# Perceiver block on one core: thirteen attention units a batch instead of fourteen, the left-over token done apart on transposed scores

## The chip, the cores and the metric

The kernel runs on one core of a Trainium2 chip. The metric is device time in microseconds (us). The engines are PE (TensorE, matmuls), ACT (ScalarE), DVE (VectorE), POOL (GpSimd) and SP (SyncE, which issues most DMAs). Each works through its own program in order and meets the others only at semaphores.

## The reference, cut to what matters

Sixteen batches. Each has 64 latents and 1601 context tokens of 128 channels. A cross attention with 16 heads reads the tokens and the latents themselves as keys; a small self attention and a mixture of experts follow, once, over all 1024 latents.

```python
x = layer_norm(ctx, g1, b1); l = layer_norm(latents, g2, b2)      # 1601 and 64 rows a batch
q = l @ Wq; k, v = split(concat([x, l]) @ Wkv)                     # 1665 keys
w = softmax((q * s) @ (k * s).T)                                    # per head, s = 64 ** -0.25
out = (w @ v) @ Wo
x = x + out                                                         # then self attention, experts
```

## The kernel before

**What is computed.** The key and value maps are folded into the queries and into the output map, so the heads share the 128-channel tokens. A batch's queries are 1024 columns (16 heads by 64 latents). Tokens lie in 13 tiles of 128: twelve full ones (`FULL`) and one of 65 rows (`REST`). The latents as keys are a unit of their own with 64 rows, since their queries are other columns of `q_hi` and `q_lo` (from `COLS` on). So a batch has 14 units: `UNITS = TILES + 1`, `LAT = TILES`. Each operand is kept as a high and a low float16 part, and each product is three matmuls: high by high, low by high, high by low.

**A unit.** `scores(turn, u)` on PE writes keys by 1024 query columns into two of the four banks of `S`, with six matmuls of 512 columns. The latent unit has two more that add the shift row (L1982). ACT turns the scores into the exponentials, first to the float16 part `p_hi` (`exponentials_high`, L1721), then in full into the bank (`exponentials_full`, L1726). DVE subtracts one from the other (`low_part`, L1429), which gives `p_lo` and frees the two banks for `scores(u + 2)`. `weigh(turn, u)` on PE multiplies by the tokens, six matmuls of 512 columns, into the two banks `OA`; the latent unit's go to the two work banks `W`.

**A slot.** One slot is one batch: `slot(b)` on each engine. PE's order in unit u is `scores(b, u)`, the early items of `PLAN[u]`, `weigh(b, u - 2)`, and the late items. The last two units of a batch are weighed in units 0 and 1 of the next slot. Items: `q` (48 matmuls of 64 columns: the next batch's queries, in four quarters), `m` (32 pieces of the first, rough score pass of the next batch, whose row maxima DVE takes; 24 long ones of 512 columns at L1942 and 8 short ones at L1944/L1945), `mt` (the maxima turned into a row), `pj` (96 matmuls, the output map of the batch before).

**Work banks.** The items take turns on two PSUM banks, `W[0]` and `W[1]`: `BANK` gives them out alternately in the order of `PLAN`. `bank_free(item)` has PE wait until the reader of the bank's item before has finished: DVE's `maxima` (L1417) for `m`, DVE's `queries_low` (L1408) for `q`, ACT's copies (L1735) for `ol`, the latent unit's output. So item n + 2 cannot start before item n was read. DVE's order in unit u is: statistics of batch b + 2 (L413, L403 to L409), `queries_low` and `maxima` of the unit's items, in unit 6 two short reciprocals (L704, L706), `low_part(b, u)`, in units 0 and 1 the high parts of batch b + 1 (L1302). ACT's is: `exponentials_high`, `queries_high` (L1707), `exponentials_full`, then in unit 0 the copy of `OA` (L1730), in unit 1 the copies of the latents' output (L1735), later the normalisation of raw tokens (L1659) and `o_hi` (L1702).

Of the kernel before, what the change touches and what calls it, by code (L numbers as in the profile page):

```python
# [29 lines left out]
UNITS = TILES + 1  # L30
LAT = TILES
HALF = COLS // 2
GROUPS = 4
# [46 lines left out]
def some(first, count):  # L80
# [7 lines left out]
        ([], []),  # L88
        ([("q", 0), ("q", 1)], some(0, 1)),
        (some(1, 2), some(3, 2)),  # L90
        ([("q", 2), ("q", 3)], some(5, 1)),
        (some(6, 2), some(8, 2)),
        (some(10, 2), some(12, 2)),
        (some(14, 2), some(16, 1)),
        (some(17, 2), some(19, 2)),
        (some(21, 2), some(23, 1)),
        (some(24, 2), some(26, 2)),
        (some(28, 2), some(30, 2)),
# [15 lines left out]
NORMALISE_AT = {6: [0], 7: [1, 2], 8: [3, 4, 5], 9: [6], 10: [7], 11: [8, 9], 12: [10, 11], 13: [12]}  # L114
RECIPROCALS_AT = 6
OUTPUTS_HIGH_AT = {10: 0, 11: 1}
PREP = ("q", "m", "mt")


def rows_of(u):  # L120
    return 128 if u < FULL else (REST if u == FULL else NQ)


def perceiver(nc, x, ctx_in, ln1_g, ln1_b, ln2_g, ln2_b, Wq, Wkv, Wo, aWq, aWk, aWv, aWo,
              lq1, lk1, lq2, lk2, rms_scale, gate_w, gate_b, expert_w, expert_b, out):
    es = ExitStack()
    with es:
# [18 lines left out]
        def part(start, size, dt=F32):  # L146
# [37 lines left out]
        lk_odd = [sb(f"lk_odd{k}", [NQ, TB, D], F16) for k in range(2)]  # L184
# [5 lines left out]
        ck_hi = [sb(f"ck_hi{p}", [NQ, D], F16) for p in range(2)]  # L190
        ck_lo = [sb(f"ck_lo{p}", [NQ, D], F16) for p in range(2)]
# [4 lines left out]
        xT_hi = [sb(f"xT_hi{p}", [128, TILES * 128], F16) for p in range(2)]  # L196
        xT_lo = [sb(f"xT_lo{p}", [128, TILES * 128], F16) for p in range(2)]
# [101 lines left out]
                   (("q", 4), ("mt", 2), ("pj", 1))}  # L299
# [3 lines left out]
                "mt": sem("m_row", 2), "ol": sem("ol_copied", 2), "pj": sem("pj_copied", 1)}  # L303
# [22 lines left out]
        def pbuf(turn, u):  # L326
            return (2 * (turn.off % 2) + u) % NPB

        def score_bank(u, half):
            return S[:, 2 * (u % 2) + half, :]  # L330
# [111 lines left out]

        def inverse_rows(sp, turn):
# [66 lines left out]
        X1_AT, H_AT, TILE0_AT, KEYS1_AT, VALUES1_AT = 2, 8, 10, 11, 12  # L510
# [31 lines left out]
        def early_variances(dve, link, u):  # L542
# [4 lines left out]
            if u == X1_AT + 1:  # L547
                for t in range(5):
                    nc.vector.bn_stats(st[:, t, :], xres[:, t, :])
# [485 lines left out]
        def tail_tensor(pe, side_item, weigh):  # L1035
# [114 lines left out]
            pe.wait_ge(lo_done.sem, lo_done.upto(LAST, TILES - 1))  # L1150
# [3 lines left out]
            weigh(LAST, TILES - 1)  # L1154
# [60 lines left out]
        def _(sp):  # L1215
# [25 lines left out]
            transposes(sp, Turn(0))  # L1241
            load_raw(sp, Turn(2))
            sp.wait_ge(lk_done.sem, 1)
            for k in range(2):
                sp.dma_start(lk_odd[k][:], lk[k][NQ:128]).then_inc(ld_lk.sem, 16)
            for b in range(B):
                if b + 1 < B:
                    transposes(sp, Turn(b + 1))
                if b + 3 < B:
                    load_raw(sp, Turn(b + 3))  # L1250
                if b + 3 == B:
                    sp.dma_start(xres[:], x.rearrange("(t j) q d -> (j q) t d", j=2)).then_inc(ld_res.sem, 16)
                if b > 0:
                    inverse_rows(sp, Turn(b - 1))
            inverse_rows(sp, LAST)
# [9 lines left out]
        def _(dve):  # L1265
# [158 lines left out]
            def low_part(turn, u):  # L1424

                r, k = rows_of(u), pbuf(turn, u)
                dve.wait_ge(e_done.sem, e_done.upto(turn, u))
                src = S[0:r, 2 * (u % 2):2 * (u % 2) + 2, :].rearrange("p a n -> p (a n)")
                nc.vector.tensor_tensor(p_lo[k][0:r, :], src, p_hi[k][0:r, :], ALU.subtract)\  # L1429
                  .then_inc(lo_done.sem, 1)  # L1430

            def slot(b, prep=True, post=True, stats=True):
                nxt = b.plus(1)
                for u in range(UNITS):
                    if stats:
                        statistics(b.plus(2), u)
                    for kind, k in PLAN[u][0] + PLAN[u][1]:
                        if kind == "q" and prep:
                            queries_low(nxt, k)
                        if kind == "m" and prep:  # L1440
                            maxima(nxt, k)
                    if u == RECIPROCALS_AT and post:
# [54 lines left out]
        def _(pool):  # L1497
# [50 lines left out]
            def at_batch(k, turn):  # L1548
                return lk_odd[k][:, turn.off // 2, :] if turn.off % 2 else lk[k][0:NQ, turn.off // 2, :]
# [8 lines left out]
            def current_k(turn):  # L1558
# [3 lines left out]
                if turn.off == 1:  # L1562
                    pool.wait_ge(ld_lk.sem, 32)
                nc.gpsimd.tensor_copy(ck_hi[p][:], at_batch(0, turn))
# [549 lines left out]
```

## Time and profile before

| | us |
|---|---|
| median of 3 runs | 997.82 (996.78 to 1000.93) |
| the profiled execution, as timed | 998.82 |
| its span in the trace | 997.1 |
| PE busy | 944.7 (95%) |
| DVE busy | 782.8 (79%) |
| ACT busy | 738.6 (74%) |
| POOL busy | 376.0 (38%) |
| one slot in the steady part | 49.53 |

The span is from the first to the last instruction. A matmul's record of 512 columns lasts 380 ns, but the next one starts 216 ns after it began: records overlap, and a PE that has stood still for up to some 160 ns still looks busy. For PE one therefore reads the starts, not the busy time. The timeline merges equal neighbours; "x2" is two matmuls, and its start is that of the first.

### The profile page before, as it was taken

What the parts mean: (1) busy time and instruction counts of PE and PEld (TensorE: products, weight loads), DVE (VectorE), ACT (ScalarE), POOL (GpSimd) and SP (SyncE); (2) the same over time, 40 slices, a digit from 0 to 9 for tenths busy, and PEclk for the clock granted to TensorE, in tenths of its full rate; (3) what the DMA queues carried; (4) which work ended last, traced back from release to release, by engine and by line L of the source; (5) the groups of instructions that cost most, each with busy time, mean ns of one, the idle gap of its engine ahead of it and who ended that gap; (6) DMA issues with size and microseconds to landing.
All of it is one profiled execution on the core that took longest, in us unless ns stands there. A gap on an engine that the chain in (4) does not pass through costs nothing.

```text
span 997.1 us, 19671 instructions
## 1 busy us (share of the span) xinstructions
PE 944.7 (95%) x7942; PEld 501.6 (50%) x7942; DVE 782.8 (79%) x1540; ACT 738.6 (74%) x1017; POOL 376.0 (38%) x376
## 2 busy tenths in 40 slices
PE   8679999999999999999999999999999998969975
PEld 5434455454545454545454545454545454547742
DVE  5968796969696969696969696969695956658965
ACT  4576878787878787878787878787878776635631
POOL 6471143433333343434343434343434223143343
PEclk9799999999999999999999999999999999979987
DMA  6212020302020312121212121121212000000000
GB/s 204 68 22 58 11 79 15 76 17 74 18 73 18 73 17 73 23 68 25 66 24 67 23 68 33 59 37 54 32 48 35 22 2 22 1 23 23 2 7 16
DMA packets 73218, 41.79 MB, mean 42 GB/s; under 512 B 60932, under 2 KB 68520, under 8 KB 73128
## 3 DMA queue, kind: packets, MB, share of 16 engines
q1 hardware_dynamic: 72840, 39.49, 16.4%
q8 instruction: 63, 1.03, 0.4%
q10 hardware_dynamic: 288, 1.05, 0.3%
q14 instruction: 27, 0.22, 0.1%
HBM read 25.98 MB, written 0.59 MB: 27 GB/s over the span
## 4 chain that ended last, share of the span: by engine, by line
PE 81%; DVE 13%; ACT 2%; issue 2%; POOL 1%; DMA 1%; POOLq 0%; ACTq 0%; DVEq 0%
PE S L1977 10%; PE S L1985 9%; PE S L1979 9%; PE OA L2006 9%; PE OA L2008 9%; PE OA L2010 9%; PE WW L1942 8%; PE WW L1958 1%; PE WW L1960 1%; DVE mx L1417 1%; PE WW L1959 1%; PE WW L1929 1%; DVE amx L720 1%; PE WW L1931 1%; PE WW L1930 1%
## 5 line engine op out<-in xcount | busy, mean ns | idle before, releaser
L1429 DVE TENSOR_TENSOR region<-S,region 128x1024 f16<-128x1024 f32 (+1 forms) x224 | 272.1, 1215 | 107.5 <-ACT S L1726 106.8
L1721 ACT ACTIVATE region<-S,sigma 128x1024 f16<-128x1024 f32 (+1 forms) x224 | 250.3, 1117 | 121.4 <-PE S L1985 121.4
L1417 DVE TENSOR_REDUCE mx<-WW 128x1 f32<-128x512 f32 (+1 forms) x480 | 263.6, 585 | 29.9 <-PE WW L1942 21.2
L1726 ACT ACTIVATE S<-S,sigma 128x1024 f32<-128x1024 f32 (+1 forms) x224 | 244.1, 1090 | 0.0
L1977 PE MATMUL S<-region,xT_hi 128*128 128x512 f16 (+1 forms) x416 | 124.3, 380 | 3.4 <-DVE region L1429 2.2
L2006 PE MATMUL OA<-region,xk 128*128 128x512 f16 (+1 forms) x416 | 124.4, 381 | 0.0
L1985 PE MATMUL S<-region,xT_lo 128*128 128x512 f16 (+1 forms) x416 | 124.2, 380 | 0.0
L2008 PE MATMUL OA<-region,xk 128*128 128x512 f16 (+1 forms) x416 | 124.2, 380 | 0.0
L1979 PE MATMUL S<-region,xT_hi 128*128 128x512 f16 (+1 forms) x416 | 124.1, 380 | 0.0
L2010 PE MATMUL OA<-region,xk 128*128 128x512 f16 (+1 forms) x416 | 124.0, 380 | 0.0
L1942 PE MATMUL WW<-xT_hi,region 128*128 128x512 f16 x360 | 120.3, 380 | 1.6 <-DVE region L1408 0.9
L1543 POOL TENSOR_TENSOR xk<-raw,xk 128x508 f16<-128x508 f32 x64 | 62.5, 996 | 143.1 <-DVE xk L1302 143.1
L461 POOL TENSOR_TENSOR region<-region,rb 128x512 f32<-128x512 f32 x32 | 40.5, 1267 | 141.2 <-DMA rb<-inv_dram 141.2
L469 POOL TENSOR_TENSOR ew<-region,o_hi 128x1024 f16<-128x1024 f32 x32 | 68.1, 2128 | 64.2 <-ACT o_hi L1702 64.2
L1659 ACT ACTIVATE raw<-raw,smc 128x128 f32<-128x128 f32 (+1 forms) x187 | 84.0, 491 | 0.0
L1532 POOL TENSOR_TENSOR smc<-smc,mhalf 128x13 f32<-128x13 f32 x16 | 38.9, 2433 | 99.1 <-DVE smc L409 99.1
L1979 PEld LDWEIGHTS S<-region,xT_hi 128*128 128x128 f16 (+1 forms) x416 | 41.2, 99 | 49.1 <-issue 0.6
L1985 PEld LDWEIGHTS S<-region,xT_lo 128*128 128x128 f16 (+1 forms) x416 | 41.2, 99 | 48.9 <-issue 0.5
L2010 PEld LDWEIGHTS OA<-region,xk 128*128 128x128 f16 (+1 forms) x416 | 40.8, 98 | 49.4 <-issue 0.6
L2008 PEld LDWEIGHTS OA<-region,xk 128*128 128x128 f16 (+1 forms) x416 | 40.7, 98 | 49.5 <-issue 0.6
L1942 PEld LDWEIGHTS WW<-xT_hi,region 128*128 128x128 f16 x360 | 35.0, 97 | 50.8 <-DVE mx L1417 13.8
L413 DVE BATCH_NORM_STATS2 stc<-raw 128x6 f32<-128x128 f32 (+1 forms) x208 | 45.6, 277 | 15.2 <-ACT raw L1659 15.2
(296 smaller groups left out, 1728.3 us busy)
## 6 DMA issues: line engine op xcount, KB each, us to landing
raw<-ctx SPq DMA_DIRECT2D x16, 768.0 KB
rb<-inv_dram SPq DMA_DIRECT2D x16, 512.0 KB, 3.6
raw<-ctx SPq DMA_DIRECT2D x16, 32.5 KB
WO_lo<-L_xattn_Wq ACTq DMA_DIRECT2D x1, 512.0 KB, 3.9
WO_hi<-L_xattn_Wkv ACTq DMA_DIRECT2D x1, 512.0 KB, 4.8
lx<-x SPq DMA_DIRECT2D x1, 512.0 KB, 5.9
region<-L_xattn_Wo SPq DMA_DIRECT2D x1, 512.0 KB, 8.0
WO_hi<-L_xattn_Wkv SPq DMA_DIRECT2D x1, 512.0 KB, 8.9
```

The source lines that it names most:

```text
L1417: nc.vector.tensor_reduce(mx[:, r, c:c + 1], W[BANK[("m", n)]][:, 0:width], AX.X, ALU.max)\
L1429: nc.vector.tensor_tensor(p_lo[k][0:r, :], src, p_hi[k][0:r, :], ALU.subtract)\
L1659: ins = nc.scalar.activation(x_[0:r, t, :], x_[0:r, t, :], ACT.Identity, bias=smc[0:r, 2, t:t + 1], scale=smc[0:r, 1, t:t + 1])
L1721: nc.scalar.activation(p_hi[k][0:r, :], src, ACT.Exp, scale=sigma[0:r, 0:1])
L1726: nc.scalar.activation(src, src, ACT.Exp, scale=sigma[0:r, 0:1]).then_inc(e_done.sem, 1)
L1942: ins = mm(w, rows, xT_hi[p][:, 512 * c:512 * c + 512], start=True, stop=True)
L1977: mm(score_bank(u, k)[0:r], hi, q_hi[p][:, cols[k]], start=True, stop=False)
L1979: mm(score_bank(u, k)[0:r], hi, q_lo[p][:, cols[k]], start=False, stop=False)
L1985: ins = mm(score_bank(u, k)[0:r], lo, q_hi[p][:, cols[k]], start=False, stop=True)
L2006: mm(dst[k], hi, ph[0:r, cols[k]], start=first, stop=False)
L2008: mm(dst[k], hi, pl[0:r, cols[k]], start=False, stop=False)
L2010: ins = mm(dst[k], lo, ph[0:r, cols[k]], start=False, stop=last)
```

## The change

- The last tile keeps 64 of its 65 tokens (`KEPT`), and these and the 64 latents form one unit of 128 rows, unit 12. `UNITS` is 13.
- In its `scores` each step is a pair of matmuls, tokens and latents, with 64 weight columns each and the results in partitions 0 to 63 and 64 to 127 of one bank. In its `weigh` each step is a pair with 64 rows each, the tokens' into `OA`, the latents' into the work banks.
- `OA` is complete only with that unit, so the weighing of unit 12 in the next slot's unit 1 stands ahead of `scores(b, 1)`, and ACT's copy of `OA` waits for it.
- The 65th token: a new item `lf` (late in unit 2) computes its scores transposed, 16 matmuls with 128 weight columns and one or two data columns. DVE adds the three parts, ACT takes the exponential twice (unit 3), DVE subtracts (unit 4), a new item `lt` (late in unit 5) turns the 16 columns into rows, ACT copies them, SP moves them by three DMAs into one tile of three rows, and `weigh_left` (unit 10) adds them to `OA` by two matmuls of 512 columns. SP also fetches three rows of the token itself.
- With one unit less, `PLAN` packs the 32 `m` items into units 3 to 11, and the normalisation and three steps of the last slot move by up to one unit. POOL's copies of the latents go to partitions 64 to 127, the banks of `S` and the `p` buffers alternate over all units instead of within a batch.

```diff
-UNITS = TILES + 1
-LAT = TILES
+UNITS = TILES
+LAT = TILES - 1
+KEPT = REST - 1
+LEFT = FULL * 128 + KEPT
...
 PLAN = [([], []),
         ([], []),
-        ([], []),
-        ([("q", 0), ("q", 1)], some(0, 1)),
-        (some(1, 2), some(3, 2)),
-        ([("q", 2), ("q", 3)], some(5, 1)),
-        (some(6, 2), some(8, 2)),
-        (some(10, 2), some(12, 2)),
-        (some(14, 2), some(16, 1)),
-        (some(17, 2), some(19, 2)),
-        (some(21, 2), some(23, 1)),
-        (some(24, 2), some(26, 2)),
-        (some(28, 2), some(30, 2)),
+        ([], [("lf", 0)]),
+        ([("q", 0), ("q", 1)], some(0, 2)),
+        (some(2, 2), some(4, 2)),
+        ([("q", 2), ("q", 3)], some(6, 1) + [("lt", 0)]),
+        (some(7, 2), some(9, 2)),
+        (some(11, 2), some(13, 2)),
+        (some(15, 2), some(17, 2)),
+        (some(19, 2), some(21, 2)),
+        (some(23, 2), some(25, 2)),
+        (some(27, 2), some(29, 3)),
         ([("mt", 0), ("mt", 1)], [("pj", 0)])]
...
-NORMALISE_AT = {6: [0], 7: [1, 2], 8: [3, 4, 5], 9: [6], 10: [7], 11: [8, 9], 12: [10, 11], 13: [12]}
+NORMALISE_AT = {6: [0], 7: [1, 2, 3], 8: [4, 5, 6], 9: [7, 8, 9], 10: [10, 11], 11: [12]}
+LEFT_EXP_AT, LEFT_LOW_AT, LEFT_AT = 3, 4, 10
...
-        X1_AT, H_AT, TILE0_AT, KEYS1_AT, VALUES1_AT = 2, 8, 10, 11, 12
+        X1_AT, H_AT, TILE0_AT, KEYS1_AT, VALUES1_AT = 2, 8, 9, 10, 11
...
+        def left_columns(sp, turn):
+            p = turn.off % 2
+            if turn.off >= 2:
+                sp.wait_ge(pv_done.sem, pv_done.upto(turn.plus(-2), LEFT_AT - 1))
+            sp.dma_start(left_x[p][0:2, :], xk[p][KEPT:REST, :, FULL, :]).then_inc(left_x_in[p].sem, 16)
+            sp.dma_start(left_x[p][2:3, :], xk_hi[p][KEPT:REST, FULL, :]).then_inc(left_x_in[p].sem, 16)
+        def left_rows(sp, turn):
+            sp.wait_ge(free["lt"].sem, free["lt"].upto(turn))
+            if turn.off > 0:
+                sp.wait_ge(pv_done.sem, pv_done.upto(turn.plus(-1), LEFT_AT - 1))
+            for k, first in enumerate((0, 0, 8)):
+                sp.dma_start(left_row[k:k + 1, :].rearrange("o (r n) -> o r n", n=128), left_pT[first:first + 8, :])\
+                  .then_inc(left_row_in.sem, 16)
...
+            def left_scores(turn):
+                dve.wait_ge(pe_item["lf"].sem, pe_item["lf"].upto(turn))
+                parts = W[BANK[("lf", 0)]][:, 0:32].rearrange("p (r c) -> p r c", c=4)[:, :, 0:3]
+                nc.vector.tensor_reduce(left_s[:], parts, AX.X, ALU.add).then_inc(free["lf"].sem, 1)
+            def left_low_part(turn):
+                dve.wait_ge(left_exp.sem, left_exp.upto(turn))
+                nc.vector.tensor_tensor(left_p[:, 8:16], left_e[:], left_p[:, 0:8], ALU.subtract)\
+                  .then_inc(left_low.sem, 1)
...
+            def left_exponentials(turn):
+                act.wait_ge(free["lf"].sem, free["lf"].upto(turn))
+                nc.scalar.activation(left_p[:, 0:8], left_s[:], ACT.Exp, scale=sigma[:, 0:1])
+                nc.scalar.activation(left_e[:], left_s[:], ACT.Exp, scale=sigma[:, 0:1]).then_inc(left_exp.sem, 1)
...
             def outputs(turn):
-                act.wait_ge(pv_done.sem, pv_done.upto(turn, TILES - 1))
+                act.wait_ge(pv_done.sem, pv_done.upto(turn, LAT))
...
+                if kind == "lf":
+                    for r in range(8):
+                        rows = slice(128 * r, 128 * r + 128)
+                        mm(w[:, 4 * r:4 * r + 2], q_hi[p][:, rows], xT[p][:, :, LEFT], start=True, stop=True)
+                        ins = mm(w[:, 4 * r + 2:4 * r + 3], q_lo[p][:, rows], xT_hi[p][:, LEFT:LEFT + 1],
+                                 start=True, stop=True)
+                if kind == "lt":
+                    pe.wait_ge(left_low.sem, left_low.upto(turn))
+                    if turn is LAST:
+                        pe.wait_ge(x1_read.sem, 1)
+                    ins = mm(w[0:16, 0:128], left_p[:], ident16[:], start=True, stop=True)
...
                 if u < LAT:
-                    hi, lo, qc = xT_hi[p][:, 128 * u:128 * u + r], xT_lo[p][:, 128 * u:128 * u + r], 0
+                    at = slice(128 * u, 128 * u + 128)
+                    keys_of = [(slice(0, 128), xT_hi[p][:, at], xT_lo[p][:, at], 0)]
                 else:
-                    hi, lo, qc = cT_hi[p][:], cT_lo[p][:], COLS
+                    at = slice(128 * u, 128 * u + KEPT)
+                    keys_of = [(slice(0, KEPT), xT_hi[p][:, at], xT_lo[p][:, at], 0),
+                               (slice(KEPT, 128), cT_hi[p][:], cT_lo[p][:], COLS)]
...
+            def weigh_left(turn):
+                pe.wait_ge(left_x_in[turn.off % 2].sem, raw_loaded(turn))
+                pe.wait_ge(left_row_in.sem, turn.times(48, 48))
+                for k in range(2):
+                    mm(OA[:, k, :], left_x[turn.off % 2][:], left_row[:, HALF * k:HALF * k + HALF],
+                       start=False, stop=False)
...
                 for u in range(UNITS):
+                    if post and u == LATENTS_AT:
+                        weigh(old, LAT)
                     scores(b, u)
                     side_items(PLAN[u][0])
...
                     elif post and u == 0:
-                        weigh(old, TILES - 1)
-                    elif post and u == LATENTS_AT:
-                        weigh(old, LAT)
+                        weigh(old, LAT - 1)
+                    if u == LEFT_AT:
+                        weigh_left(b)
```

## Rows read from the trace of the kernel before

**Rows 1.** The page's chain of work that ended last, shares by engine.
```profile
PE 81%; DVE 13%; ACT 2%; issue 2%; POOL 1%; DMA 1%; POOLq 0%; ACTq 0%; DVEq 0%
```
**Rows 2.** One steady slot: window, length, busy of PE, PEld, DVE, ACT, POOL; clock.
```profile
405.69:455.22 49.53, 49.48 (x411) 24.95 (x412) 40.61 (x78) 40.88 (x54) 18.90 (x18) 1.00 0.19 46
```
**Rows 3.** Timeline of PE (start, length, line, tiles), units 6 and 7.
```profile
484.79 0.19 PE L1944 MATMUL WW<-xT_hi,region 128*128 128x65 f16 x1
...
485.06 0.39 PE L1942 MATMUL WW<-xT_hi,region 128*128 128x512 f16 x1
485.28 0.59 PE L1977 MATMUL S<-region,xT_hi 128*128 128x512 f16 x2
...
486.58 0.38 PE L1942 MATMUL WW<-xT_hi,region 128*128 128x512 f16 x1
...
488.23 0.60 PE L1942 MATMUL WW<-xT_hi,region 128*128 128x512 f16 x2
```
**Rows 4.** Timeline of PE, unit 13: mt, weighing (then pj), the next slot's first scores.
```profile
506.75 0.61 PE L1950 MATMUL WW<-ident,m 128*1 128x128 f16 x8
507.30 0.61 PE L2006 MATMUL OA<-region,xk 128*128 128x512 f16 x2
...
511.40 0.60 PE L1977 MATMUL S<-region,xT_hi 128*128 128x512 f16 x2
```
**Rows 5.** Timeline of PE in setup and tail: row halves, column halves, full array.
```profile
53.17 1.16 PE L1881 MATMUL OA<-region 64*128 64x128 f32 x16 [0.45 <-ACT region L1694]
...
875.55 1.08 PE L1022 MATMUL WW<-wvaT,xk 128*64 128x256 f32 x8
876.56 1.09 PE L1063 MATMUL OA<-ident,region 128*128 128x128 f32 x8
```
**Rows 6.** Timeline of PE's weight loads in the tail, column halves.
```profile
852.20 0.36 PEld L1022 LDWEIGHTS WW<-wvaT,xk 128*64 128x64 f32 x4
```
**Rows 7.** Timeline of ACT: copies in units 1 and 3, exponentials of unit 7.
```profile
468.28 1.11 ACT L1735 COPY region<-WW 128x512 f32<-128x512 f32 x2
...
472.36 1.06 ACT L1707 CAST region<-WW 128x512 f16<-128x512 f32 x2
...
486.78 1.11 ACT L1721 ACTIVATE region<-S,sigma 128x1024 f16<-128x1024 f32 x1 [1.02 <-PE S L1985]
487.79 1.08 ACT L1726 ACTIVATE S<-S,sigma 128x1024 f32<-128x1024 f32 x1
```
**Rows 8.** Timeline of DVE, units 3 to 7 of one slot.
```profile
472.97 1.29 DVE L1408 TENSOR_TENSOR region<-WW,region 128x512 f16<-128x512 f32 x2
...
474.87 1.22 DVE L1429 TENSOR_TENSOR region<-S,region 128x1024 f16<-128x1024 f32 x1
476.00 0.68 DVE L1417 TENSOR_REDUCE mx<-WW 128x1 f32<-128x512 f32 x1
...
479.83 0.17 DVE L403 TENSOR_TENSOR smc<-stc 128x13 f32<-128x13 f32 x1
...
480.79 1.28 DVE L1408 TENSOR_TENSOR region<-WW,region 128x512 f16<-128x512 f32 x2
...
486.09 0.16 DVE L704 TENSOR_SCALAR rinv<-rcol 128x8 f32<-128x8 f32 x1
...
486.40 1.17 DVE L1429 TENSOR_TENSOR region<-S,region 128x1024 f16<-128x1024 f32 x1
487.49 0.88 DVE L1417 TENSOR_REDUCE mx<-WW 128x1 f32<-128x512 f32 x2
488.66 1.29 DVE L1417 TENSOR_REDUCE mx<-WW 128x1 f32<-128x512 f32 x2 [0.28 <-PE WW L1942]
```
**Rows 9.** Timelines of SP and POOL: the row of inverses sent out, its first reader.
```profile
487.92 0.33 SPq L450 DMA_DIRECT2D rb<-inv_dram  x1
...
491.60 1.26 POOL L461 TENSOR_TENSOR region<-region,rb 128x512 f32<-128x512 f32 x1 [7.91 <-DMA rb<-inv_dram]
```
**Rows 10.** Timeline of PE, last slot, unit 8.
```profile
836.36 1.75 PE L560 MATMUL WW<-ident,raw 128*128 128x128 f32 x7 [3.32 <-DVE raw L579]
```

## What the change does to the time: the prediction

> **What bounds the kernel now.** I read the chain of work that ended last first: 81% of it is PE, 13% DVE [rows 1]. The table by stretches confirms it for a steady slot: of 49.53 us PE is busy in 49.48, DVE in 40.61, ACT in 40.88, at a granted clock of 1.00, the 2.4 GHz level [rows 2]. That invites a sum over PE alone, and the sum alone would be wrong. The starts in the timeline show why. In unit 6 the short m item 8 starts at 484.79 and takes 0.06 (two small matmuls); the long m item 9 could follow at 484.85 and starts at 485.06 [rows 3]. PE waited 0.21 for a work bank, hidden in the busy time, since records of 380 ns cover gaps of up to 0.16. In unit 7 item 12 could start at 486.58 + 0.22 + 0.06 + 1.30 = 488.16 and starts at 488.23 [rows 3]: DVE's reading of items 10 and 11 began at 487.49 and the long one ended some 0.68 later, at 488.17 [rows 8]. So PE is the bound, but with only a few tenths of slack towards DVE, because item n + 2 waits until DVE has read item n, and DVE has `low_part` in between. These two waits, 0.29, are what a slot loses now.
>
> **Prices.** `scores` or a full `weigh`: 1.30 (485.28 to 486.58), a long m 0.22 [rows 3]. A matmul of 64 columns: pj's 96 lie between 507.30 + 1.30 and 511.40, 0.029 each; so q's pair of quarters is 1.40 and a short m 0.06. Changing the array's shape: eight mt matmuls of 0.055 are 0.44, the next weighing starts 0.55 after the first, so 0.10 [rows 4]. ACT starts 0.20 after `scores` ends (486.58, 486.78), the second exponential 1.01 later, 1.08 long: the exponentials are ready 2.29 after `scores`; a bank copy is 0.6 with 0.48 between starts [rows 7]. DVE: from an m's start on PE to its reader 0.43 (488.23, 488.66), 0.61 from one long reader or q reader to the next and 0.68 long, a short one 0.20; `low_part` 1.13 to the next start, 1.22 long; the two reciprocals 0.31; the statistics' seven steps 0.96 [rows 3, 8]. A bank goes back to PE some 0.05 after its reader.
>
> **Part 1, PE's work.** One unit goes: scores and weighing, 2 x 1.30 = 2.59 less. The joint unit has six pairs for scores, two matmuls for the shift row, six pairs for weighing. If a pair costs what one matmul costs, it is as long as the latent unit was, changes of shape included. Do pairs overlap? For rows: sixteen records of 128 columns on alternate row halves take 1.16, 0.073 each; eight of 128 columns on the full array take 1.09, 0.136 each. For columns: eight records of twice as many columns, 256, on alternate column halves take 1.08, no longer than the eight of 128 [rows 5]. Both overlap fully, so a pair is 0.22.
>
> The loads of two column halves with a duration of 0.14 each begin together, four within 0.36 [rows 6]. The Trainium skill, "TensorE: Matmul & The Clock Gate", Part 3, says that a weight load overlaps with running matmuls only where the row group differs; tokens and latents share all row groups in `scores`, so by that rule each pair would fall apart and the sum would be that of the second rival below. The trace's rows just named speak against it.
>
> Added on PE: `lf`, sixteen small matmuls, 0.029 each by the nearest row (64 columns with new weights), 0.055 by the mt row, so 0.47 to 0.88; I take 0.47, and part 2 shows that up to 0.7 costs the same. `lt` 0.055 and two changes of shape, 0.25. `weigh_left`, 2 x 0.216 and two changes (three rows instead of 128), 0.63; without changes 0.43. Sum: -2.59 + 0.47 + 0.25 + 0.63 = -1.24 a slot.
>
> **Part 2, PE's waits.** I lay the new order out with the prices above, unit by unit.
> - A, units 1 to 3. The weighing of the joint unit now stands ahead of `scores(1)`, not behind. After `scores(1)` PE has only `scores(2)` and `weigh(0)`, 2.60, then `lf`. `lf` needs the bank of `ol`: ACT copies it at 2.29 - 0.1, ready 2.86. It ends at 3.33. `scores(3)` needs `low_part(1)`: 2.29 + 0.03 + 1.22 + 0.05 = 3.59. Without waits it were 3.07: 0.52 lost. Up to now the latents' weighing covered this.
> - B, unit 3. There are two late m items, not one; the second takes q1's bank. From the end of `scores(3)`: ACT's first exponential starts at 0.3 (it has the copies and unit 2's exponentials before it), q1's high part ends at 0.3 + 1.0 + 0.47 + 0.59 = 2.36; DVE reads q0 from 1.92, q1 from 2.53 to 3.21, bank free at 3.26. PE is there at 1.40 + 1.30 + 0.22 = 2.92: 0.34.
> - C, unit 4. DVE runs on: m0, m1, `low_part(3)` to 5.49, m2, m3 to 6.79; m5 waits until 6.84, PE is there at 6.73: 0.11.
> - D, unit 5, from the start of `scores(5)`: `lt` takes q3's bank. DVE: m4, m5 and the left-over's low part to 1.2, `low_part(4)` to 2.33, statistics to 3.29, q2, q3 to 4.58, free 4.63. PE is there at 1.30 + 1.40 + 1.30 + 0.22 = 4.22: 0.41.
> - E, unit 7, from late item m9: DVE starts at 0.43, m10 1.04, reciprocals 1.65, `low_part(6)` 1.96, m11 3.09, m12 3.29 to 3.97. m14 needs m12's bank, 4.02. PE is there at 0.43 + 1.30 + 0.28 + 1.30 + 0.22 = 3.53: 0.49.
> - F, unit 11, from m25: DVE 0.43, m26 1.04, `low_part(10)` 1.24, m27 2.37, m28 2.98 to 3.66. m30 at 3.71, PE at 0.28 + 1.30 + 0.43 + 1.30 + 0.06 = 3.37: 0.34.
> Sum 2.21; the 0.29 of now are replaced. I checked the other units the same way and found nothing above 0.05. ACT loses two exponentials and gains four tiny instructions; its fullest unit has two exponentials, one `o_hi` and two normalisations as before. DVE loses 1.13 and gains some 0.3. POOL's copies keep their size.
>
> **The moved DMAs.** The three row DMAs stand on SP behind the row of inverses, issued 1.5 after DVE's reciprocals; DVE comes to these some 2.4 later in the slot, about 28.5 us after its start. With 0.33 each to issue and the 3.7 that the inverses needed to land [rows 9] they are in by 33.5; `weigh_left` comes at 38.7. Five microseconds of cover. The inverses' reader, POOL, then finishes 3 us before `o_hi` asks. The two DMAs for the token's rows delay the raw load by 0.7, which has a whole slot.
>
> **Sum.** A steady slot: -1.24 + 2.21 - 0.29 = +0.68, thirteen of them (1 to 13): +8.8. Slot 14 has no statistics, so D is gone: +0.3. Slot 0 has no A, the rest balances its saving: 0. Last slot: before unit 8 PE stands 3.3 for DVE [rows 10], and DVE's step there hangs on unit 7's scores, which come later by `lf`, A and `lt`, 1.2; behind it a unit less and `weigh_left`, -1.96; so -0.7. Together +8.4 on 998.8 of the profiled execution: 1007.2. The median of three is 1.0 below that execution, so 1006.5 (rounded), against 997.8.
>
> **Rivals.**
> First, the waits don't come and PE's work decides: DVE finds the reads early enough, or its order gives slack that my layout misses. For it: 81% of the chain is PE, and DVE has 9 us spare in a slot. Against it: the two waits in units 6 and 7, which the prices reproduce. All gone: -1.24 - 0.29 in 15 slots and -1.2 in the last, with the 0.29 staying or gone, 974 to 978. Half of them gone: -1.24 + 1.1 - 0.29, -0.4 a slot, about 991. The point from which the kernel is faster: waits under 1.5 a slot. This is the rival on the other side.
> Second, the column pairs of `scores` run one after another: 6 x 0.216 = 1.30 a slot, +21, about 1027; the row pairs as well, 1048. Against it: rows 5 and 6, though their operands are float32 and the two halves of `L1022` share their data columns, which these don't.
> Third, `weigh_left` waits for its row. Beyond 5 us of delay each microsecond costs one a slot; with 1 us too late, about 1020. The profile gives no sign of a queue that slow.
> Fourth, the change does what it says but the delays feed each other, through ACT's copies in units 1 to 3 above all: 0.5 more a slot, 1014.
>
> **How the numbers follow.** Forecast (1001 to 1012) 0.58; half of the waits 0.14; none or few 0.12; delays that feed each other 0.08; pairs apart 0.05; rows late 0.03. About 0.5% is what can be told from no change, so below 992.8 is faster: 0.12 and some 0.06 of the half case. Between 992.8 and 1002.8: the rest of the half case and the low edge of the forecast, 0.16. Slower: 0.66. The range 990 to 1018 leaves out some 0.13 below and 0.07 above; the likeliest case has 1001 to 1012.
>
> **What would show it.** Starts on PE: `scores(3)` 3.6 after the end of `scores(1)` (A); m1 0.3 behind m0's end (B); `lt` 0.4 behind m6 (D); m14 0.5 behind m13 (E); m30 0.3 behind m29 (F). A pair's starts a few ns apart and pairs 0.216 apart. A steady slot of 50.2. Wrong it would be if the slot is under 49.2, if the pairs are 0.43 apart, or if `lf` takes over 0.7.

## The result and the profile after

| | before | after |
|---|---|---|
| median, us | 997.81 | 1005.76 (1005.16 to 1006.42, 4 runs) |
| ratio | | 1.009 (95%: 1.0056 to 1.0125) |
| profiled execution, span | 998.82, 997.1 | 1005.16, 1003.4 |
| steady slot | 49.53 | 50.07 |

The kernel is slower by 0.9%. PE does less, and the slot is longer all the same. From the page after: the first row with the engines' busy time, then the chain of work that ended last, which answers to [rows 1].

```profile
PE 936.7 (93%) x8246; PEld 488.8 (49%) x8246; DVE 760.4 (76%) x1556; ACT 720.4 (72%) x1033; POOL 376.7 (38%) x376
PE 56%; DVE 29%; ACT 8%; issue 5%; POOL 1%; DMA 1%; POOLq 0%; ACTq 0%; DVEq 0%
```

PE's share of the chain fell from 81% to 56%, DVE's rose from 13% to 29%, ACT's from 2% to 8%: the chain now leaves PE several times a slot. One slot, in the columns of [rows 2] (window, length, busy of PE, PEld, DVE, ACT, POOL, granted clock, DMA share, GB/s):

```profile
465.34:515.41 50.07, 49.01 (x435) 24.21 (x432) 39.20 (x79) 39.80 (x54) 18.95 (x17) 1.00 0.20 45
```

Every engine but POOL has less to do than in [rows 2], at the same clock of 1.00. The waits stand in PE's starts. The timeline of PE, this slot, in five places (start, length, line, tiles; in brackets the idle time that the records show and what ended it):

```profile
471.60 0.59 PE L2075 MATMUL S<-region,xT 128*128 128x512 f16 x2
...
473.60 0.18 PE L2020 MATMUL WW<-xT,region 128*128 128x2 f16 x1
...
473.99 0.16 PE L2021 MATMUL WW<-xT,region 128*128 128x1 f16 x1
474.34 0.61 PE L2066 MATMUL S<-region,xT 128*128 128x512 f16 x2 [0.18 <-DVE region L1469]
...
478.34 0.38 PE L2012 MATMUL WW<-xT,region 128*128 128x512 f16 x1
478.91 0.39 PE L2012 MATMUL WW<-xT,region 128*128 128x512 f16 x1 [0.18 <-DVE region L1448]
...
486.69 0.39 PE L2012 MATMUL WW<-xT,region 128*128 128x512 f16 x1
487.29 0.22 PE L2027 MATMUL WW<-ident,left_p 128*16 128x128 f16 x1 [0.20 <-DVE region L1448]
487.44 0.60 PE L2066 MATMUL S<-region,xT 128*128 128x512 f16 x2
...
493.69 0.39 PE L2012 MATMUL WW<-xT,region 128*128 128x512 f16 x1
494.29 0.20 PE L2014 MATMUL WW<-xT,region 128*128 128x65 f16 x1 [0.21 <-DVE mx L1457]
...
507.79 0.20 PE L2015 MATMUL WW<-cT_hi,region 128*128 128x64 f16 x1
508.16 0.61 PE L2012 MATMUL WW<-xT,region 128*128 128x512 f16 x2 [0.17 <-DVE mx L1457]
```

`scores(1)` ends at 470.73 (the step behind it starts there), and L2066 of unit 3 comes at 474.34, 3.61 later; `lf` itself stood 0.27 for a work bank (it could start at 473.33). A long `m` needs 0.22, so m1 stood 0.35, `lt` 0.38 and m14 0.38 behind the `m` ahead of them; m30 stood 0.33. The name in each bracket is the DVE reader whose bank was wanted.

### The profile page after: what moved, and what is told of

It reads as the page before. It is cut to its first block, busy times and chain, and to the rows that moved or that the text cites. A ratio compares the mean times of both kernels' runs of the same rounds, so it can differ in the third digit from the quotient of the medians.

```text
span 1003.4 us, 20455 instructions
## 1 busy us (share of the span) xinstructions
PE 936.7 (93%) x8246; PEld 488.8 (49%) x8246; DVE 760.4 (76%) x1556; ACT 720.4 (72%) x1033; POOL 376.7 (38%) x376
## 4 chain that ended last, share of the span: by engine, by line
PE 56%; DVE 29%; ACT 8%; issue 5%; POOL 1%; DMA 1%; POOLq 0%; ACTq 0%; DVEq 0%
DVE mx L1457 8%; DVE region L1469 7%; PE S L2066 6%; PE WW L2012 6%; PE OA L2099 6%; PE S L2075 6%; PE S L2069 6%; PE OA L2102 6%; PE OA L2105 6%; DVE region L1448 4%; ACT S L1781 2%; ACT region L1777 2%; ACT region L1801 2%; PE WW L2039 1%; PE WW L2041 1%
## 5 line engine op out<-in xcount | busy, mean ns | idle before, releaser
L1469 DVE TENSOR_TENSOR region<-S,region 128x1024 f16<-128x1024 f32 x208 | 252.8, 1215 | 139.1 <-ACT S L1781 139.0
L1777 ACT ACTIVATE region<-S,sigma 128x1024 f16<-128x1024 f32 x208 | 232.6, 1118 | 131.6 <-PE S L2075 130.4
L1457 DVE TENSOR_REDUCE mx<-WW 128x1 f32<-128x512 f32 (+1 forms) x480 | 259.7, 584 | 42.0 <-PE WW L2012 37.6
L1781 ACT ACTIVATE S<-S,sigma 128x1024 f32<-128x1024 f32 x208 | 226.2, 1088 | 0.0
L2066 PE MATMUL S<-region,xT 128*128 128x512 f16 (+1 forms) x416 | 124.5, 381 | 6.0 <-DVE region L1469 4.7
L2012 PE MATMUL WW<-xT,region 128*128 128x512 f16 x360 | 121.3, 382 | 6.2 <-DVE region L1448 3.7
L2075 PE MATMUL S<-region,xT 128*128 128x512 f16 (+1 forms) x416 | 125.0, 382 | 0.0
L2069 PE MATMUL S<-region,xT 128*128 128x512 f16 (+1 forms) x416 | 124.5, 381 | 0.0
L1715 ACT ACTIVATE raw<-raw,smc 128x128 f32<-128x128 f32 (+1 forms) x187 | 80.9, 489 | 0.0
L2012 PEld LDWEIGHTS WW<-xT,region 128*128 128x128 f16 x360 | 34.9, 97 | 66.1 <-DVE mx L1457 22.7
L2075 PEld LDWEIGHTS S<-region,xT 128*128 128x128 f16 (+1 forms) x416 | 40.0, 99 | 52.5 <-issue 7.7
L2069 PEld LDWEIGHTS S<-region,xT 128*128 128x128 f16 (+1 forms) x416 | 41.1, 99 | 48.6
L1999 PE MATMUL WW<-cT_hi,G_hi 128*128 128x64 f16 x512 | 50.0, 195 | 3.0 <-issue 3.0
```

What stands on the lines that cost most here:

```text
L1457: nc.vector.tensor_reduce(mx[:, r, c:c + 1], W[BANK[("m", n)]][:, 0:width], AX.X, ALU.max)\
L1469: nc.vector.tensor_tensor(p_lo[k], src, p_hi[k], ALU.subtract).then_inc(lo_done.sem, 1)
L1715: ins = nc.scalar.activation(x_[0:r, t, :], x_[0:r, t, :], ACT.Identity, bias=smc[0:r, 2, t:t + 1], scale=smc[0:r, 1, t:t + 1])
L1777: nc.scalar.activation(p_hi[k], src, ACT.Exp, scale=sigma[:, 0:1])
L1781: nc.scalar.activation(src, src, ACT.Exp, scale=sigma[:, 0:1]).then_inc(e_done.sem, 1)
L2012: ins = mm(w, rows, xT_hi[p][:, 512 * c:512 * c + 512], start=True, stop=True)
```

## The experiments

All times are medians, and a ratio is against the kernel before. That one was run beside each group: 997.6, 997.1, 995.2 and 996.5 in the four groups, single executions between 993 and 1002. A slot read from the trace is therefore the sharper measure of an edit; from slot 2 to slot 13 it repeats within 0.02 unless said otherwise, and it is compared with the 50.07 of the kernel after.

### The column pairs

```diff
-for k in range(2):
-    for r, hi, lo, qc in keys_of:
-        mm(banks[r, k, :], hi, q_hi[p][:, cols(qc, k)], ...)
+for r, hi, lo, qc in keys_of:      # all six matmuls of the tokens, then the latents' six
+    for k in range(2):
+        mm(banks[r, k, :], hi, q_hi[p][:, cols(qc, k)], ...)
```

> In the joint unit's scores all matmuls of the tokens come first, then all of the latents, so no two neighbours but one lie in different column halves. Same work. If pairs overlap only as neighbours: 11 steps for 6, 5 x 0.216 = 1.08 us a slot more, 17 us in 16 slots, about 1023 us. If pairs never overlapped, or the order does not matter: 1005.8 us.

Measured: 1012.62, ratio 1.0159 (1.0122 to 1.0197), slot 50.53, so +0.46 on 50.07 where 1.08 was expected. Timeline of PE in unit 12, first of the kernel after, then of this run; in this run L2066 and L2068 are the steps with the high keys and L2073 those with the low keys, and the program has the six of `xT` ahead of all of `cT`.

```profile
508.70 0.40 PE L2066 MATMUL S<-region,xT 128*64 128x512 f16 x1
508.70 0.40 PE L2066 MATMUL S<-region,cT_hi 128*64 128x512 f16 x1
508.94 0.38 PE L2066 MATMUL S<-region,xT 128*64 128x512 f16 x1
508.94 0.38 PE L2066 MATMUL S<-region,cT_hi 128*64 128x512 f16 x1
509.15 0.38 PE L2069 MATMUL S<-region,xT 128*64 128x512 f16 x1
...
510.78 0.33 PE L2031 MATMUL WW<-ident,m 128*1 128x128 f16 x3
```

```profile
511.92 0.62 PE L2066 MATMUL S<-region,xT 128*64 128x512 f16 x2
512.38 0.38 PE L2068 MATMUL S<-region,xT 128*64 128x512 f16 x1
512.38 0.40 PE L2066 MATMUL S<-region,cT_hi 128*64 128x512 f16 x1
512.59 0.38 PE L2068 MATMUL S<-region,xT 128*64 128x512 f16 x1
512.62 0.38 PE L2066 MATMUL S<-region,cT_hi 128*64 128x512 f16 x1
...
513.91 0.62 PE L2073 MATMUL S<-region,cT_lo 128*64 128x512 f16 x2
```

In the kernel after the halves of a pair start within 0.01 of each other and the whole block, from 508.70 to 510.78, is 2.08. In this run the seventh matmul of the program, `cT`'s first, starts with the third, ahead of the fourth. Two of `xT` run alone at the beginning and two of `cT` at the end, so the block has two steps more, 2 x 0.216 = 0.43, and not the five that the text above expected; measured it is 2.54, 0.46 more. Overlap of column halves is real, and it also happens out of program order. Why the seventh is taken then, and how far it could be moved ahead, no run shows.

The Trainium skill, "TensorE: Matmul & The Clock Gate", Part 3, says that matmuls start and end strictly in the order of the program and that weight loads overlap only between different row groups. For column halves these rows show neither the order nor that limit: all of them use all 128 rows, the seventh matmul starts ahead of the fourth, and a pair, with a weight load for each half, comes 0.22 behind the pair before.

### What the token costs

```diff
-([], [("lf", 0)]),
+([], []),
...
-([("q", 2), ("q", 3)], some(6, 1) + [("lt", 0)]),
+([("q", 2), ("q", 3)], some(6, 1)),
```

`weigh_left`, the token's DMAs and its steps on DVE and ACT are gone as well; one token of 1601 is missing from the result.

> The left-over token is not added at all (its scores, its turning, its two matmuls and its DMAs are gone), so the output lacks one key of 1601; everything else is the changed kernel. Theory of the record (PE waits for banks and for the low parts): the unit-3 scores still come 3.6 us after the end of unit 1's (wait A takes the place of the item), the turning item's 0.38 us wait and 0.16 us of its own go, the two matmuls with 0.63 us go: 1.2 us a slot less, about 987 us. Rival (PE's work decides, waits are small): 0.40 + 0.16 + 0.63 = 1.2 us too, but then with 0.6 us less waiting in units 1 to 3. The two differ in the trace: by the theory PE stands 1.0 us ahead of unit 3's scores, by the rival it does not.

Measured: 990.4, ratio 0.9929 (0.9903 to 0.9955), slot 49.03; 987 was expected. The token costs 1.04 a slot and not 1.2. PE's start behind `lf`'s old place:

```profile
464.02 0.61 PE L2059 MATMUL S<-region,xT 128*128 128x512 f16 x2 [0.85 <-DVE region L1466]
```

`weigh(0)` ends at 463.00 and `scores(3)` waits 1.02: `lf`'s 0.40, its own wait and the gap behind it lie entirely in a wait that is there without it, as the theory has it and the rival has not. The 1.04 are `weigh_left` with its changes of shape, 0.63, and `lt`'s place, 0.04 ahead of m6 and 0.38 + 0.06 + 0.10 behind it, 0.58 together, less 0.17 that comes back in unit 10 (unit 11's 0.33 is 0.34 here): 1.04.

### DVE's readers

```diff
-nc.vector.tensor_reduce(mx[:, r, c:c + 1], W[BANK[("m", n)]][:, 0:width], AX.X, ALU.max)
+nc.vector.tensor_reduce(mx[:, r, c:c + 1], W[BANK[("m", n)]][:, 0:width // 2], AX.X, ALU.max)
```

Each maximum is taken over half of its columns.

> DVE reads only half of the columns of each maximum (the shift row is taken from half of the rough scores; all else is computed in full). PE's program is that of the changed kernel. Theory (bank waits behind DVE): the waits in units 4, 7 and 11 go (0.06 + 0.45 + 0.33 us), the one in unit 5 shrinks from 0.38 to about 0.1; those of units 1 to 3 stay (0.6 and 0.35): 1.1 us a slot less, about 989 us. Rival (PE's work decides): no change, 1005.8 us.

Measured: 993.47, ratio 0.9963 (0.9945 to 0.998), slot 49.32, so -0.75; 989 was expected. PE's starts say which waits were DVE's readers: the 0.06 in unit 4 and the 0.45 in units 6 and 7 are gone, the 0.04 + 0.38 at `lt` became 0.26, and those ahead of `scores(3)` (0.27 and 0.35) and m1 (0.35) stayed to 0.01. So A and B don't hang on the maxima; C and E do. F had been expected to go and did so only by name: m30 no longer waits, but m31 behind it waits 0.27 for the bank of m29, two items ahead. DVE had stood idle for 0.79 before it read m29. What is left there is the way from PE to DVE and back, and not a DVE that is late.

Reciprocals ahead of unit 6's maxima on DVE, not behind:

```diff
+if u == RECIPROCALS_AT and post:
+    reciprocals(dve, b.plus(-1))
 for kind, k in PLAN[u][0] + PLAN[u][1]:
```

> DVE does the two short reciprocals at the start of unit 6 instead of after the unit's maxima, where they stand in the chain that ends in unit 7's wait. Theory: that wait falls from 0.45 to 0.14 us in slots 1 to 15, 4 us in all, about 1001.5 us. Rival (the unit-7 wait comes from the number of reads, not from what is in the chain): no change.

Measured: 1005.52, ratio 1.0081 (1.0049 to 1.0113), slot 49.96. The waits of unit 7 fell from 0.45 to 0.17, as the theory has it, but 0.15 came back in unit 8, ahead of m18, and the slot fell by only 0.11: an edit of 0.3 on DVE is worth a third of that. The expected 1001.5 was wrong; the median is as without the edit.

`lt` first in unit 5, ACT copying it ahead of unit 5's exponentials:

```diff
-([("q", 2), ("q", 3)], some(6, 1) + [("lt", 0)]),
+([("lt", 0), ("q", 2), ("q", 3)], some(6, 1)),
```

> The item that turns the left-over token's column stands first in unit 5, ahead of the two quarters of the queries, instead of last, and ACT copies it before unit 5's exponentials. Theory: its wait of 0.38 us for the bank of the last quarter goes, its change of shape, hidden in that wait until now, costs 0.10: 0.3 us a slot less, 5 us, about 1001 us. Rival (PE only waits somewhere else): no change.

Measured: 999.58 (997.17 to 1002.74, 10 runs), ratio 1.0024 (1.0005 to 1.0044), slot 49.78 in all but one, which has 49.92. D is gone: `lt` stands 0.13 ahead, 0.09 behind, changes of shape included. The trace has 3.4 less in the span (1000.0 against 1003.4), the medians 6; the sizes differ by no more than the executions of one kernel do, and the sign is clear. This is the cheapest repair of the change, and it reaches the time before only nearly.

### Units 1 to 3

`weigh(old, LAT)` back behind `scores(1)`, ACT's copy of `OA` with the `ol` copies behind unit 1's exponentials:

```diff
-if post and u == LATENTS_AT:
-    weigh(old, LAT)
 scores(b, u)
...
+elif post and u == LATENTS_AT:
+    weigh(old, LAT)
```

> The joint unit is weighed behind unit 1's scores, as before the change, and ACT copies OA after unit 1's exponentials. Theory: the 0.62 us of waiting ahead of and behind the left-over token's item in unit 2 goes, but PE now waits about 0.5 us for ACT's copy of OA before the first weighing: 0.1 us a slot, about 1004 us. Rival (the order alone costs what wait A costs): 0.55 us a slot, about 997 us.

Measured: 1003.8 (1000.63 to 1006.02), ratio 1.007 (1.0047 to 1.0093), slot 49.94, so -0.13. `scores(3)` no longer waits, but `weigh(0)` ahead of it does, for ACT:

```profile
471.84 0.59 PE L2098 MATMUL OA<-region,xk 128*128 128x512 f16 x2 [0.41 <-ACT region L1796]
```

It could start at 471.26, so 0.58 stand where 0.61 stood. Of the other waits m1's and `lt`'s are about 0.1 shorter and m5's 0.1 longer. The same with DVE making that copy, to take it off ACT:

```diff
+dve.wait_ge(pv_done.sem, pv_done.upto(b.plus(-1), LAT))
+nc.vector.tensor_copy(o_sb[:, 0, :], OA[:].rearrange("p a n -> p (a n)"))\
+  .then_inc(oa_free.sem, 1)
```

> As x5_order_back, but DVE, which stands idle there, copies OA instead of ACT. Theory: the first weighing waits no more than 0.2 us, and unit 3's scores come 0.4 us earlier than in the changed kernel: 6 us, about 999.5 us. Rival (DVE's reads in units 3 to 11 are late because DVE is full, and 1.1 us more work on it comes back there): no gain, about 1005 us.

Measured: 1017.28, ratio 1.0214 (1.0188 to 1.024), slot 50.85; 999.5 was expected. DVE's timeline:

```profile
476.58 0.76 DVE L1342 CAST xk<-raw 128x508 f16<-128x508 f32 x2 [0.72 <-PE WW L2107]
477.26 0.67 DVE L432 BATCH_NORM_STATS2 stc<-raw 128x6 f32<-128x128 f32 x3
477.85 1.21 DVE L1497 COPY region<-OA 128x1024 f32<-128x1024 f32 x1
```

PE's, `weigh(0)`:

```profile
479.20 0.59 PE L2101 MATMUL OA<-region,xk 128*128 128x512 f16 x2 [1.33 <-DVE region L1497]
```

The copy could start behind the joint weighing, at about 476.4. It stands in DVE's line behind the casts and the statistics, 1.4, and lasts 1.21 itself; PE waits 1.49 for its end. I had counted the 1.21 and not the line. The three edits (reciprocals, `lt` first, this copy) together:

> x3_lt_first, x4_recip_first and x6_copy_on_dve together. If the waits are separate, their gains add: 0.3 + 0.13 + 0.4 = 0.8 us a slot, 12 us, about 993 us, faster than the kernel before. If one wait passes on to the next, less: 0.5 us a slot, about 998 us.

Measured: 1009.83, ratio 1.0141 (1.0114 to 1.0168), slot 50.60. `weigh(0)` again waits 1.49, and neither sum came true. Against the run before, the slot is 0.26 shorter: `lt`'s wait of 0.33 is gone for a second change of shape, 0.09, and in units 7 and 8 the 0.45 became 0.17 + 0.15, with 0.08 ahead of m9. The two small edits are worth less together than their 0.30 and 0.11 alone.

`q0` moved ahead of `scores(3)`, to cover A with work:

```diff
-([], [("lf", 0)]),
-([("q", 0), ("q", 1)], some(0, 2)),
+([], [("lf", 0), ("q", 0)]),
+([("q", 1)], some(0, 2)),
```

> The kernel after, with one side item moved: the quarter q0 stands behind lf in unit 2, ahead of scores(3), and no longer behind it. It lasts 0.70, and the gap ahead of scores(3) is 0.34 behind lf, with lf itself standing 0.27 for the bank of ol. Theory (the wait of term A is the time of low_part(1), which nothing on PE covers): the gap ahead of scores(3) is 0, a steady slot is 0.3 to 0.6 shorter, median 998 to 1002. Rival (DVE and ACT are late by themselves in units 1 to 3, and the order on PE only moves where it shows): the gap comes back ahead of q1, m1 or scores(4), as long as before, and the median stays at 1005 to 1007.

Measured: 1012.27, ratio 1.0165 (1.0133 to 1.0197), slot 50.60, so +0.53. The rival's direction, and worse than the rival. DVE's timeline:

```profile
480.39 0.69 DVE L1448 TENSOR_TENSOR region<-WW,region 128x512 f16<-128x512 f32 x1 [0.95 <-ACT region L1763]
481.00 1.22 DVE L1469 TENSOR_TENSOR region<-S,region 128x1024 f16<-128x1024 f32 x1
482.13 0.47 DVE L432 BATCH_NORM_STATS2 stc<-raw 128x6 f32<-128x128 f32 x2
482.52 0.67 DVE L1448 TENSOR_TENSOR region<-WW,region 128x512 f16<-128x512 f32 x1
```

PE's, m0 and m1:

```profile
481.90 0.38 PE L2012 MATMUL WW<-xT,region 128*128 128x512 f16 x1
483.25 0.39 PE L2012 MATMUL WW<-xT,region 128*128 128x512 f16 x1 [0.96 <-DVE region L1448]
```

`scores(3)` now starts 0.03 behind the last matmul of q0, and q0 0.08 behind `lf`: of A only `lf`'s own 0.27 is left. But DVE stands 0.95 for q0's copy, which ACT makes behind unit 2's exponentials, with `low_part(2)` queued behind it. q1 is read at 482.52, as long after `scores(3)` as in the kernel after, while PE reaches m1 0.7 sooner: it waits 1.13.

So both quarters ahead, DVE reading them behind `low_part(2)`, with `lt` first:

```diff
+([], [("lf", 0), ("q", 0), ("q", 1)]),
+([], some(0, 2)),
...
 low_part(b, u)
+if u == 2 and prep:
+    queries_low(nxt, 0)
+    queries_low(nxt, 1)
```

> The kernel with lt first in unit 5, and besides both quarters q0 and q1 behind lf in unit 2, ahead of scores(3); DVE reads them behind low_part(2), not ahead of it. In the run with q0 alone moved, DVE stood 0.95 for q0's copy with low_part(2) queued behind it, and m1 waited 1.13. Laid out from that run's rows, with lf's end as 0: q0 and q1 to 1.5; ACT copies q0 to 2.5, q1 to 3.0; DVE's low_part(2) ends at 3.2, q0 is read to 3.8, q1 to 4.5; PE is at m0 at 4.1 and at m1 at 4.3, which waits 0.2. Theory (the wait goes if the work moved ahead of scores(3) covers low_part(1) and its readers don't stand behind one another): 0.69 of waits in units 2 and 3 become 0.3, some 0.3 to 0.4 a slot less than with lt first alone (999.6), so 995 to 996. Rival (scores(3) is itself 0.8 later, and low_part(3) and what hangs on it carry the delay into units 4 and 5): m5, q2 or m6 wait instead, 999 to 1003.

Measured: 1007.01, ratio 1.0105 (1.0078 to 1.0132), slot 50.37 in all but one, which has 50.50; 995 to 996 was expected. The waits ahead of `scores(3)` and m1 are gone. A new one, 0.88, stands between q0 and q1: q1 is due at 477.52.

```profile
478.39 0.20 PE L2002 MATMUL WW<-cT_hi,G_hi 128*128 128x64 f16 x1 [0.72 <-DVE left_s L1474]
```

q1's bank is the one that `lf` wrote, and DVE's timeline shows its reader, L1474:

```profile
475.79 1.23 DVE L1469 TENSOR_TENSOR region<-S,region 128x1024 f16<-128x1024 f32 x1 [1.62 <-ACT S L1784]
476.93 0.55 DVE L1342 CAST xk<-raw 128x508 f16<-128x508 f32 x2
477.39 0.86 DVE L432 BATCH_NORM_STATS2 stc<-raw 128x6 f32<-128x128 f32 x4
478.18 0.16 DVE L1474 TENSOR_REDUCE left_s<-WW 128x8 f32<-128x24 f32 x1
```

`lf` ended at 476.73, and its reader stands behind casts and statistics until 478.18. I had laid out the banks of `q` and `m` and forgotten `lf`'s. The 0.69 of waits in units 2 and 3 became 0.96. That is less than half of the loss: the slot is 0.6 longer than with `lt` first alone. The rest is the rival's, m5 in unit 4:

```profile
485.79 0.39 PE L2015 MATMUL WW<-xT,region 128*128 128x512 f16 x1 [0.21 <-DVE mx L1457]
```

It stands 0.38, with 0.04 ahead of m4, where it stood 0.06. So both causes are there, the bank that was forgotten and the delay passed on. It was not tried with the reading of `lf` moved ahead of the casts.

### The statistics

```diff
-STATS_AT = {0: range(0, 4), 1: range(4, 7), 2: range(7, 11), 3: range(11, 13)}
-COMBINE_AT = 5
+STATS_AT = {0: range(0, 5), 1: range(5, 9), 2: range(9, 13)}
+COMBINE_AT = 3
```

> The kernel after, with the statistics of the batch after next taken five, four and four tokens' tiles in units 0 to 2, and their combination in unit 3, where it was four, three, four and two with the combination in unit 5. DVE has 0.96 less ahead of the reading of q2 and q3. Theory (term D is that reading, delayed by the combination): the 0.38 ahead of lt go, and the slot is 0.17 (as slot 14, which has no statistics, against its neighbours) to 0.42 shorter, median 1000.5 to 1003.5. Rival (DVE's backlog only changes its place): the waits ahead of scores(3) and m1 grow by as much, median 1005 to 1009.

Measured: 1051.08, ratio 1.0553 (1.0524 to 1.0583), slots of 52.5 to 54.2. Far outside both. The timelines of DVE, POOL and PE:

```profile
498.90 2.15 DVE L422 TENSOR_TENSOR smc<-stc 128x13 f32<-128x13 f32 x1
500.97 0.17 DVE L423 TENSOR_TENSOR smc<-stc 128x13 f32<-128x13 f32 x1
```
```profile
498.67 2.34 POOL L491 TENSOR_TENSOR srow<-region 1x1024 f32<-1x1024 f32 x1
```
```profile
502.58 0.39 PE L2012 MATMUL WW<-xT,region 128*128 128x512 f16 x1 [2.36 <-DVE region L1448]
```

Windows of the same stretch (length, busy of PE, PEld, DVE, ACT, POOL, granted clock, DMA share, GB/s):

```profile
501.00:503.40 2.40, 0.61 (x2) 0.23 (x3) 2.30 (x10) 0.08 (x1) 1.40 (x2) 0.96 1.00 190
503.40:505.00 1.60, 1.60 (x5) 0.59 (x4) 1.49 (x3) 0.00 (x0) 1.25 (x2) 0.50 0.94 387
505.00:506.60 1.60, 1.60 (x6) 0.50 (x5) 0.65 (x1) 0.22 (x1) 0.00 (x0) 0.50 0.13 30
506.60:510.00 3.40, 3.40 (x22) 1.63 (x21) 2.76 (x6) 1.88 (x2) 0.00 (x0) 1.00 0.00 0
```

L422 subtracts 13 numbers a partition from 13 others, both in SBUF, and lasts 2.15; the same kind of instruction behind it lasts 0.17. It ends when POOL's L491 ends, at 501.0. The grouped lines (count, busy, mean ns of one, idle ahead), of this run and then of the kernel after, have all 16:

```profile
L422 DVE TENSOR_TENSOR smc<-stc 128x13 f32<-128x13 f32 x16 | 28.6, 1786 | 0.1
```
```profile
L422 DVE TENSOR_TENSOR smc<-stc 128x13 f32<-128x13 f32 x16 | 2.8, 174 | 0.1
```

Of the 16, the 13 that overlap L491 last 2.14 to 2.25, and each ends 0.04 behind it; the other three last 0.17. In the kernel after the combination comes in unit 5, clear of L491: in the slot shown above L491 starts at 477.0 and L422 at 485.0. m0 waits 2.53, of which 2.0 are the lengthened L422; the other 0.5, by an estimate, come with the seven steps themselves, 0.96 by their price, which now stand ahead of the reading of q0. Then a second cost: in this slot, after these 2.5 us of standing and 0.38 more, the clock fell from 2.4 to 1.2 GHz (0.50) for 3.4 us, and matmuls started 0.43 apart. In the slot before, 52.5 long, it did not fall, with the same two stands. It fell in nine of the thirteen slots with these stands, and these nine are 1.6 longer.

The Trainium skill, "SBUF — State Buffer", section "SBUF: two separate sides", has the first: a GpSimd instruction and a VectorE one with two SBUF inputs lock a shared pair of ports for a whole instruction, and the other blocks. The trace agrees: the VectorE instruction loses 2.0.

The wait that the edit was meant for, D, did not go either. It fell from 0.42 to 0.26, as with half maxima, and as in slot 14 of the kernel after, which has no statistics. What is left there is ACT's, whose high parts of q2 and q3 DVE now stands for:

```profile
457.57 1.29 DVE L1448 TENSOR_TENSOR region<-WW,region 128x512 f16<-128x512 f32 x2 [0.70 <-ACT region L1763]
```

The same statistics with `q0` ahead of `scores(3)` and `lt` first in unit 5, as in the runs of these edits alone:

> Three edits of order in the kernel after at once: q0 ahead of scores(3), lt first in unit 5, the statistics early. All three are about waits at different places, A and D. Theory (each wait is a local lateness of one reader and goes by itself): 0.55 for A and 0.42 for D a slot, less what slot 0 and the last don't give, 12 to 13 us, so 993 to 994, a little faster than the kernel before, with E and F (0.8 a slot) still there. Rival (what is taken away in units 2 to 5 comes back in 7 to 11): 998 to 1001, no faster than before.

Measured: 1033.07, ratio 1.037 (1.0342 to 1.0399). It is far outside both as well, for the same combination in unit 3, and PE stands 2.58 ahead of m1. But L491 starts 1.34 ahead of L422 here, not 0.23, and L422 lasts 1.04, again to the end of L491: it lasts as long as L491 has still to go. In the slots in which the clock did not fall, the slot is 51.74, against 52.47 with the statistics alone and 50.60 with q0 alone; the wait ahead of `lt` is gone.

## Why the prediction was right, point by point

**PE's work.** Forecast -1.24 a slot, measured -2.59 + 0.40 + 0.16 + 0.63 = -1.40. The pairs run as forecast (508.94, 509.15: a pair every 0.22). `lf` is 0.40 and not 0.47: sixteen matmuls with one or two data columns at 0.025 each, less than the 0.029 of 64 columns. `weigh_left` is 0.44 and two changes of 0.10 and 0.09, as forecast. `lt`, 0.06, has one change of 0.10 behind it; the one ahead of it falls into the wait.

**The waits.**

| | forecast | measured | evidence |
|---|---|---|---|
| A, `scores(3)` | 0.52 | 0.61 (0.27 + 0.34) | 0.34 of it covered by q0 in one run, and replaced |
| B, m1 | 0.34 | 0.35 | untouched by shorter maxima |
| C, m5 | 0.11 | 0.06 | gone with half maxima |
| D, `lt` | 0.41 | 0.42 (0.04 + 0.38) | gone with `lt` first; 0.26 of it stays when DVE is early |
| E, m13, m14 | 0.49 | 0.45 (0.07 + 0.38) | gone with half maxima |
| F, m30 | 0.34 | 0.33 | 0.27 one item later with half maxima |

Sum 2.22, forecast 2.21. The slot by the terms: -1.40 + 2.22 - 0.29 = +0.53; by the trace +0.54. The forecast was +0.68: the work was forecast too dear, by `lt`'s first change of shape (0.09) and by `lf` (0.07). That the sum of the waits is right to 0.01 is in part luck: A is 0.09 longer, C and E are 0.09 shorter.

A's price, 3.59 from the end of `scores(1)` to `scores(3)`, measured 3.61, and the reading of it holds: DVE stands 1.62 ahead of `low_part(1)`, waiting for ACT.

```profile
473.06 1.23 DVE L1469 TENSOR_TENSOR region<-S,region 128x1024 f16<-128x1024 f32 x1 [1.62 <-ACT S L1781]
```

It is not that DVE is full, but that the way PE, ACT, DVE, PE takes 3.6 and PE has 3.0 to do meanwhile. Without `lf` the wait is 1.02 and `scores(3)` comes as late.

**Other slots.** Slots 1 to 14 together grew by 7.5, forecast 8.8 + 0.3 = 9.1. For slot 14 the reason was wrong: without the statistics D is not gone, 0.26 of it stay for ACT's copy of the queries, which the layout of D leaves out; the slot grew by 0.39. Slot 0 changed by -0.1 (forecast 0), the setup by -0.25 (not counted), the stretch from the last slot's start to the end by -0.8 (forecast -0.7). Together +6.3 in the span against the forecast 8.4.

The last slot's sum was right with wrong parts. Unit 8's `early_columns` [rows 10] start 0.8 later after the slot's start than before, where the layout had 1.2; behind them PE needs 1.6 less to the end and not 1.96. And there is a wait that no step had: `pj` of the last slot now comes before POOL has made `o_low` for it.

```profile
862.45 0.19 PE L2039 MATMUL WW<-o_hi,WO_hi 128*128 128x64 f16 x1 [1.16 <-POOL ew L505]
```

PE stands 1.33 there. I checked the inverses' way to POOL only for the steady slots.

**The median.** The profiled execution moved from 998.82 to 1005.16, +6.3, the medians from 997.81 to 1005.76, +7.95. The forecast took 1.0 between execution and median; after it was -0.6, on the other side. 1006.5 owes some of its closeness to this: too much in the slots, too little here.

**The rivals.** The first (waits don't come) fell with the five stands above; the price of waits from which the kernel would be faster, 1.5 a slot, was right in kind, and 1.7 with the work as measured (1.40 + 0.29): with half maxima they are 1.50 (0.62, 0.35, 0.26, 0.27), the slot is 49.32 and the time is 0.9963 of before. The second (pairs apart) fell with the starts of a pair; even split by hand the order costs 0.46, not 1.08. The third (the row comes late): no wait ahead of `weigh_left` beyond the change of shape, 0.10. The fourth, delays that feed each other, did not show in the kernel after, whose waits are each close to what was laid out, but it is what the repairs met: m1 with q0 ahead, m5 with both quarters ahead, m18 with the reciprocals ahead.

## What to carry to other kernels

When work is taken out of an engine that is the bound by a few tenths only, lay the order out anew with starts from the trace, bank by bank; the waits that the shorter order uncovers (here 2.22 a slot) can exceed the work saved (1.40). A wait of a chain through three engines goes only if other work covers it without standing in any of their lines: ask for every moved instruction what is queued ahead of it, what is queued behind it, and who reads its bank, the small items' banks too. A step may look free on an idle engine and still be moved onto a neighbour's lock; compare its duration before and after the move.

## What the runs showed of the hardware

- Matmuls on different column halves overlap fully, all 128 rows in use (a pair every 0.22), and also out of the order of the program: the seventh started with the third.
- Sixteen matmuls, each with new weights of 128 columns and with one or two data columns, take 0.40: 0.025 each, hardly less than with 64 data columns (0.029).
- A change of shape costs 0.09 to 0.10 and vanishes where PE stands anyway (`lt` starts 0.06 after its bank's reader ends, with a change ahead of it).
- A DVE subtraction on 13 numbers a partition, both operands in SBUF, took 2.15 in place of 0.17 beside a POOL instruction of 2.34 on one partition that began 0.23 ahead of it, and 1.04 beside one that began 1.34 ahead: it ended with the POOL instruction each time.
- After 2.5 us of standing and 0.38 more the granted clock was 0.50 for 3.4 us in nine of thirteen slots, and stayed at 1.00 in the other four with the same stands.
